# Sparse experts in two phases, tiles turned by DMA flips, one register read per tile

## The reference

```python
x = x + tanh(g_xattn) * attention(layernorm(x), ctx)   # self and cross attention, 16 heads, 8 groups, quantised projections
z = layernorm(x).reshape(2048, 256)
scores = softmax(z @ gate_w.T)                          # 8 experts
topk_w, topk_idx = top_k(scores, 2); topk_w /= topk_w.sum()
y = sum over the 2 experts of topk_w * (silu(z @ w1[e]) * (z @ w3[e])) @ w2[e]    # inner width 176
shared = silu(z @ sw1) * (z @ sw3) @ sw2                # inner width 352
x = x + tanh(g_ffn) * (y + shared)
```

## Time and profile before

| what | value |
|---|---|
| median of 3 runs | 1025.54 us (1023.68 to 1028.03) |
| the profiled execution's own time | 1025.76 us |
| its span, first to last instruction | 1023.9 us |
| mean granted TensorE clock | 0.939 |
| busy share: PE, PEld, DVE, ACT, POOL | 83%, 62%, 76%, 74%, 71% |
| DMA moved | 80.01 MB, mean 78 GB/s |

### The profile page before, as it was taken

The page is one execution under the profiler, slowest core; times in us unless marked ns, Lnnn a source line. Parts: engine busy times, 40 slices in busy tenths (PEclk is TensorE's granted clock), DMA queues, the critical chain, the costliest instruction groups (busy, mean ns, idle before and its releaser), DMA issues. The chain is left out here.

```text
span 1023.9 us, 20898 instructions
## 1 busy us (share of the span) xinstructions
PE 850.3 (83%) x6339; PEld 630.0 (62%) x6339; DVE 778.5 (76%) x1748; ACT 759.8 (74%) x2450; POOL 723.5 (71%) x560
## 2 busy tenths in 40 slices
PE   0475899999999999999999999999866647777841
PEld 0354677777787778777777877778633425555420
DVE  8899888889888898988988888898665764333134
ACT  3486899999999999999999999999772314444210
POOL 4597789799889888888978989888632223332265
PEclk9697899999999999999999999999987769999975
DMA  9423224243333324233332424233534112222134
GB/s 247 106 83 104 57 52 78 53 77 63 62 66 65 73 51 87 51 72 66 61 67 52 87 51 77 62 64 64 145 65 111 53 31 89 91 85 83 47 98 128
DMA packets 191351, 80.01 MB, mean 78 GB/s; under 512 B 168876, under 2 KB 185356, under 8 KB 191308
## 3 DMA queue, kind: packets, MB, share of 16 engines
q1 hardware_dynamic: 183788, 68.07, 29.4%
q0 software_dynamic: 7520, 11.41, 4.7%
HBM read 30.30 MB, written 9.31 MB: 39 GB/s over the span
## 5 line engine op out<-in xcount | busy, mean ns | idle before, releaser
L1609 POOL TENSOR_TENSOR rstd<-var,mhalf 128x8 f32<-128x8 f32 (+1 forms) x128 | 191.2, 1510 | 76.6 <-DVE var L1201 76.2
L386 PE MATMUL A<-w_hi,xq 128*128 128x256 f16 (+1 forms) x1024 | 188.0, 250 | 35.7 <-DVE v_lo L1175 21.2
L387 PE MATMUL A<-w_lo,xq 128*128 128x256 f16 (+1 forms) x1024 | 187.9, 250 | 0.0
L483 PE MATMUL S<-kT,qT 128*128 128x256 f32 x512 | 142.5, 403 | 12.3 <-ACT kT L874 8.9
L1187 DVE TENSOR_SCALAR qT<-T,qmap 128x512 f32<-128x512 f32 x128 | 103.5, 809 | 55.9 <-PE T L454 55.9
L1159 DVE TENSOR_REDUCE nmx<-S 128x2 f32<-128x512 f32 (+1 forms) x192 | 114.8, 598 | 27.8 <-PE S L483 25.6
L885 ACT ACTIVATE prob<-S,nmx 128x256 f32<-128x256 f32 x256 | 119.7, 483 | 14.6 <-DVE nmx L1159 13.5
L386 PEld LDWEIGHTS A<-w_hi,xq 128*128 128x128 f16 x1024 | 101.4, 99 | 46.9 <-issue 30.2
L1673 POOL TENSOR_TENSOR raw<-raw,rstd 128x1024 f32<-128x1024 f32 x64 | 126.5, 1976 | 0.0
L1657 POOL TENSOR_TENSOR prob<-prob,rl 128x1024 f32<-128x1024 f32 x64 | 121.0, 1890 | 0.0
L483 PEld LDWEIGHTS S<-kT,qT 128*128 128x128 f32 x512 | 90.4, 195 | 45.9 <-ACT kT L874 19.4
(11 more groups left out here) (250 smaller groups left out, 2395.9 us busy)
## 6 DMA issues: line engine op xcount, KB each, us to landing
stage<-wallT SPq DMA_DIRECT2D x8, 1024.0 KB, 5.1
yd<-psrc SPq DMA_DIRECT2D x39, 128.0 KB, 1.7
wp<-wpT POOLq DMA_DIRECT2D x1, 2048.0 KB, 30.9
zd<-zf SPq DMA_DIRECT2D x8, 256.0 KB, 2.4
out<-xs SPq DMA_DIRECT2D x8, 256.0 KB
xs<-x SPq DMA_DIRECT2D x1, 1792.0 KB, 21.2
raw<-w13T SPq DMA_DIRECT2D x2, 704.0 KB
sq<-w13T SPq DMA_DIRECT2D x2, 704.0 KB
```

The lines of the kernel that those rows point to most:

```text
L386: nc.tensor.matmul(o, l, w_hi[:, c, col:col + n], start=(c == 0), stop=False)
L387: last = nc.tensor.matmul(o, l, w_lo[:, c, col:col + n], start=False, stop=(c == HC - 1))
L483: last = nc.tensor.matmul(o[:, t * S:(t + 1) * S], qT[:, p, 0, h, t * P:(t + 1) * P], kT[:, p, 0:S], start=True, stop=True)
L1609: return nc.gpsimd.tensor_tensor(dst, src, mhalf[:, 0:n], ALU.pow)
```

## The change

The last batch is taken out of the common plan. **Phase 0** plans, gathers and runs the rows of the first seven batches (NT0 = 35 tiles); **phase 1** those of the last (NT1 = 11 tiles), planned while the tiles of phase 0 run. So there are 46 tiles instead of 39. `yd` becomes two DRAM tensors, one per phase, so that the gathers of the first seven batches' outputs wait for tile 34 and not for the last tile.

**Rows as f16 pairs.** The normalised rows are split before they are stored: ACT's `tail_high` now reads `zf` (which shares `z`'s buffer) and POOL's new `tail_low` subtracts; the pair `zr` is turned by one DMA transpose of 8 blocks and stored to `zd`, 1 KB per row as before (`turn_z(tb)` on SP). PE's `transpose_tokens(zf)` and its waits go.

**Tiles turned by DMA.** Per tile SP issues `flip_z` (4 blocks of 128x128, f16) after the gather, `flip_a` (4 blocks; inner widths 128 and 48 instead of 88 and 88) after silu and the pair split in SBUF, and `store_y`. The PE transposes, `high_z` and `low_z` go. Rings: 6 gathers, 4 flipped z, 3 activation pairs, 4 flipped activations, 4 outputs. The down matmuls follow the up matmuls by DL = 4 tiles.

**One register read.** PE reads the expert number of tile j+1 after `expert_up(j)` and keeps the register until `expert_down` of that tile.

**Order.** POOL's wait for the last attention step ahead of `shared_low(0)` goes (the pair's buffer moved); ranks, tile counts and marks 0 to 7 move into the last attention ticks; `ffn_low(1)` moves two ticks later. In the second half `shared_low` runs on DVE, and POOL issues the 32 output gathers with nothing between them. `mix` no longer waits for `finish`. w2 is padded to 128 rows per half.

```diff
+NT0, NT1 = ((2 * P * n + E * (P - 1)) // P for n in (NE, ST))
+NTL = NT0 + NT1
+PHASES = ((0, NE, 0, NT0), (NE, NT, NT0, NT1))
+DL = 4
...
+            def turn_z(tb):
+                done(sp, ta_lo, tb)
+                sp.dma_start_transpose(zT[:, tb * ST:(tb + 1) * ST, :, :].rearrange("p t k n -> p (t k) n"),
+                                       zr[:, :, :, :].rearrange("p t k h -> p (t k h)")).then_inc(zr_read, 16)
+                sp.dma_start(zd[tb * S:(tb + 1) * S, :].rearrange("(t p) n -> p t n", p=P), zr[:, :, :, :].rearrange("p t k h -> p t (k h)")
+                             ).then_inc(zr_read, 16)
+
+            def flip_z(j):
+                landed(sp, ld_zg, j)
+                done(sp, e_up, j - 4)
+                sp.dma_start_transpose(zt[:, j % 4, :, :], zg[:, j % 6, :]).then_inc(ld_zt[j % 4], 16)
+
+            def flip_a(j):
+                done(sp, e_al, j)
+                done(sp, e_dn, j - 4)
+                sp.dma_start_transpose(at[:, j % 4, :, :], ea[:, j % 3, :, :].rearrange("p k n -> p (k n)")).then_inc(ld_at[j % 4], 16)
+
+            def store_y(j):
+                done(sp, e_y, j)
+                sp.dma_start((yd[0][j * P:(j + 1) * P, :] if j < NT0 else yd[1][(j - NT0) * P:(j - NT0 + 1) * P, :]), yo[:, j % 4, :]).then_inc(st_y[j % 4], 16)
...
+            turn_z(B - 1)
+            for j in range(3): flip_z(j)
+            for j in range(NTL + DL + 1):
+                if j + 3 < NTL: flip_z(j + 3)
+                if j < NTL: flip_a(j)
+                if j - DL + 1 >= 0 and j - DL + 1 < NTL: store_y(j - DL + 1)
...
+            def load_expert(j):
+                if j in (0, NT0):
+                    done(pe, f_idx, j // NT0)
+                which[j] = pe.value_load(expert[0:1, j:j + 1], min_val=0, max_val=E - 1)
...
+            for m in range(3, M0): shared_down(m)
+            load_expert(0)
+            for j in range(NTL + DL):
                 if j < NTL: expert_up(j)
+                if j + 1 < NTL: load_expert(j + 1)
+                if j >= DL: expert_down(j - DL)
+                if j == 2:
+                    pe.wait_ge(zr_read, 16 + 32 * B)
+                    done(pe, d_x1, B - 1)
+                    logits(NE, NT, JB, R_LG - NE * E).then_inc(f_lgm, 1)
+                if j == 7: rank(1)
+                if j == 12:
+                    for t in range(NE, NT): table(1, t)
+                if j == 16: pick_tokens(1)
...
             def high_a(j):
+                done(act, e_a, j)
+                landed(act, ld_at, j - 3)
+                nc.scalar.activation(ea[:, j % 3, 0, 0:I], ap[:, j % 2, :], ACT.Copy).then_inc(e_ah, 1)
...
+            for j in range(NTL + DL):
                 if j < NTL: expert_silu(j)
+                if j >= DL: read_y(j - DL)
+                if j < NTL: high_a(j)
...
             residual(B - 1)
             tail1(B - 1)
-            for t in range(4, 8): marks(t)
+            for t in range(8, NE): marks(t)
+            plan_tiles(0)
             shared_mul(3)
+            read_table(0)
             ffn_low(2)
-            for t in range(8, 12): marks(t)
+            read_tokens(0)
             finish(0)
             ffn_low(3)
...
+            for j in range(NTL):
+                expert_mul(j)
+                low_a(j)
+                if j == 3:
+                    read_logits(1, NE, NT, JB, R_LG - NE * E)
+                    best(1, NE, NT, 0)
+                if j == 4:
+                    best(1, NE, NT, 1)
+                    members(NE, NT)
+                if j == 8: ranks(1)
+                if j == 9:
+                    count_tiles(1)
+                    for t in range(NE, NT): marks(t)
+                if j == 10: plan_tiles(1)
+                if j == 13: read_table(1)
+                if j == 17: read_tokens(1)
+                if j == 18: slots(1)
+                if j == 19: mix_weights(1, NE, NT)
...
-            done(pool, mm_core, STEPS - 1)
             for m in range(3): shared_low(m)
             tail(B - 1)
+            tail_low(B - 1)
             for m in range(3, M0): shared_low(m)
-            exps(1, NE, NT)
-            for j in range(NTL): fetch_z(j)
-            shared_low(M0)
-            shared_low(M0 + 1)
-            for i in range(2 * NT):
-                fetch_y(i)
-                if i % 6 == 3 and M0 + 2 + i // 6 < MS: shared_low(M0 + 2 + i // 6)
+            for j in range(NTL):
+                fetch_z(j)
+                if j == 16: exps(1, NE, NT)
+            for i in range(2 * NT): fetch_y(i)
```

More of the change, by code:

```diff
@@ L657, in rank_late @@
-            def rank_late():
-                done(pe, f_m, 1)
-                for t in range(NE, NT):
-                    nc.tensor.matmul(VB[:, R_CNT:R_CNT + E], all_, member(t, t + 1), start=False, stop=False, skip_group_check=True)
-                rank(VB, NE, NT, False).then_inc(f_rk, 1)
-            def table(t):
+                    nc.tensor.matmul(o(t + 1, t1).rearrange("p (t e) -> p t e", e=E), all_, again(t, t1 - t - 1), start=False,
+                                     stop=False, skip_group_check=True)
@@ L664, in table @@
+                for t in range(t0, t1):
+                    last = nc.tensor.matmul(bank[:, R_CNT:R_CNT + E], all_, member(t, t + 1), start=False, stop=False,
+                                            skip_group_check=True)
+                last.then_inc(f_rk, 1)
+            def table(p, t):
                 done(pe, f_oh, t)
-                if t == 0:
-                    done(pe, a_core, STEPS - 1)
                 for k in range(2):
-                    last = nc.tensor.matmul(VB[:, R_TAB:R_TAB + P], ring[:, t % NR, k, 1, :], ring[:, t % NR, k, 0, :],
-                                            start=(t == 0 and k == 0), stop=False, skip_group_check=True)
+                    last = nc.tensor.matmul((T0, JB)[p][:, R_TAB:R_TAB + P], ring[:, t % NR, k, 1, :], ring[:, t % NR, k, 0, :],
+                                            start=False, stop=False, skip_group_check=True)
@@ L999, in _ @@
                     tick(b, g)
-            def high_z(j):
-                done(act, e_zt, j)
-                done(act, e_up, j - 2)
-                nc.scalar.activation(zt[:, j % 2, 0, :], (JB, VB)[j % 2][:, 0:H], ACT.Copy).then_inc(e_zh, 1)
             def expert_silu(j):
@@ L1260, in tick @@
                         low_px(n0 - 3, par(3))
+                        ranks(0)
+                        count_tiles(0)
                         shared_mul(1)
-                        mix_weights(0, 0, NE)
+                        for t in range(4): marks(t)
                     if g == 3:
@@ L1573, in _ @@
[L1573 to L1588 removed]
+            slots(0)
@@ L1602, in _ @@
             finish(3)
-            for q in range(6, NT // 2): mix(q)
+            for q in range(5, NT // 2): mix(q)
         @block.gpsimd
```

366 lines of the change are left out of this document (153 added, 213 removed).

## The result

The changed kernel took 1043.01 us (median of 4 runs, 1040.05 to 1043.42) beside 1024.97 us for the kernel before in the same measurement: 1.0157 times the time before, 95% interval 1.0139 to 1.0175. The prediction of 989 us (966 to 1018) was wrong in sign and size. The profiled execution has a span of 1041.3 us.

The account below looks back on a forecast made before the run. SP's queue was taken to bound the tile loop at 2.6 us a tile. 1023.9 - 1 + 1.5 - 19 + 13 - 31.6 = 986.8 us of span, plus 1.9 us outside it, gave 989 us, range 966 to 1018.

Parts of the forecast that it names:

- SP's queue: Tile loop: two flips of 1.08 us, a store of 0.32 us and three gaps of 0.05 us, 2.6 us a tile.
- issue equals data: Tile loop: the 20-block flip issues as long as its data takes, so fixed part 0.59 us, 0.123 us a block.
- C: Tile loop, SP's queue: a flip's issue is mostly fixed; at 1.6 us a flip, 1037 us; chance 0.06.
- B: Tile loop: DMA engines or landings decide, 3.1 us a tile, 1012 us; chance 0.17.
- A: Tile loop: PE decides, 2.2 us a tile, 970 us; chance 0.15.
- D: End: the phases do not overlap the end, which keeps some 55 us; 1008 us; chance 0.05.
- The start: Before the tile loop: first up matmul at 820 us, 19 us earlier; 814 to 831.
- the terms for the attention and `turn_z`: Attention: fewer PE transposes gain 1 us; the new 8-block turn in SP's queue costs 1.5 us.
- The gathers under the last tiles: Last seven tiles of the loop: output gathers share the DMA engines, +2 us.
- The way from the last up to the last down: End of the tile loop: four downs and the last activation's way, 5.5 us.
- The end: After the last down: 36 us instead of 67.6, DVE's chain longest, a gain of 31.6 us; 34 to 42.

Follow-up runs that it names:

- the kernel with pairs: Changed kernel with each DMA flip turning two tiles at once and flip_z issued ahead of flip_a; 0.9681 of the kernel before.
- e7_pe_turns_a: Changed kernel with the activations turned by TensorE instead of flip_a, tokens still by flip_z; 0.9673 of the kernel before.
- e9_z_pairs_pe_a: As e7_pe_turns_a, with flip_z turning two tiles at once; 0.9606 of the kernel before, 986.43 us.
- e1_hold: Changed kernel with the first sixteen output gathers waiting for the store of tile 45 instead of tile 34; 1.0065 of the kernel before.
- e3_actstore: Changed kernel with each tile's store issued by ScalarE's queue instead of SP's; 0.9780 of the kernel before.

## Why the prediction was wrong, point by point

**SP's queue, the step that failed.** The prediction found the right bound (SP, ahead of PE and the DMA engines) and gave it 2.6 us a tile; it is 3.23, and 0.5 of the 0.6 us between are two terms that were too small, about half each. The store was taken at 0.32 us, though the row of a plain DMA that follows a flip said 0.59: behind a flip it takes 0.57 us. And the flip: one size was known, 3.06 us for 20 blocks, and the line through it was drawn by an argument (issue equals data, so a fixed part of 0.59 us). Measured are 1.19 to 1.22 us for 4 blocks, 1.23 to 1.28 for 8 in the loop (1.32 in `turn_z`; predicted 1.57), 3.06 for 20. A fixed part and a slope do not fit the three sizes. 20 blocks cost 0.153 us each, 8 at that rate 1.22 us, and 4 cost nearly as much as 8: a floor near 1.2 us fits all three. The rest of the 0.6 us are the gaps between issues, 0.25 us a tile for 0.15. The text gave +41 us for 3.2 us a tile; measured are +39.5. (Its figure for 2.2 us a tile is 13 - 18.4, so -5 and not -6.) The 46 tiles up to the last up matmul take 148.0 us, where the terms sum to 124.6, and the way behind it 8.6 for 5.5. The loop is 26.5 of the 35 us between the predicted span of 986.8 and 1021.9; the start is 5 and the end 3.5 (below).

**The rivals.** C had the mechanism, a flip's issue that blocks do not pay for, with a chance of 0.06. Its break-even of 3.4 us a tile was about right: at 3.29 us the kernel is 0.2% faster. B (DMA engines or landings) had a period near the measured one, 3.1 us, but by another way: they were not the bound of the changed kernel. The DMA engines are the likely next one. Its size was nearly right: 2.2 us a tile predicted, 1.04 x 2.40 = 2.5 us in the kernel with pairs. Against 0.32 x 2.76 = 0.9 us in the one without flips that is 0.20 us for each of the 8 blocks, where 0.17 was taken from the 20-block flip. A (PE decides, 2.2 us) shows only in stretches of e7_pe_turns_a and e9_z_pairs_pe_a (2.24 and 2.25 us), and there PE does four turns a tile besides. D did not occur: 16 gathers ran under the last tiles. The sentence of the Trainium skill that starting a DMA takes little beside the DMA itself ("DMA: Bandwidth & Descriptors", "Issuing engines are not separate DMA queues") does not hold for this loop: moving 0.57 us of issue per tile to another engine's queue was worth 20 us.

**The start.** Predicted 820, measured 825.8, inside 814 to 831; with the terms for the attention and `turn_z`, -18.5 us were predicted and -13.5 measured. POOL's last `shared_low` ended at 819.7, where about 815 was assumed (820 less 5.1), and gather and flip took 5.9 us and not 5.1:

```profile
818.55 1.15 POOL L1731 TENSOR_TENSOR w_hi<-zq,w_hi 96x512 f16<-96x512 f32 x1 [0.71 <-ACT w_hi L807]
...
819.87 1.12 POOL L1738 DMA_INDIRECT w_lo<-zd,w_lo  x1 [0.18 <-issue]
...
822.79 5.03 SPq L358 DMA_TRANSPOSE psrc<-w_lo  x3
...
825.75 0.47 PE L411 MATMUL S<-w_hi,psrc 128*128 x1 [4.51 <-DMA psrc<-w_lo]
```

**The loop's other terms.** The gathers under the last tiles were priced at 2 us and cost 5 (e1_hold). The way from the last up to the last down was priced at 5.5 us; it is 8.6, as the last `flip_a` takes 5.2 us to land (3.5 at the median) where 2.5 was taken.

**The end.** Predicted 36 us (34 to 42), measured 39.5, and 49 in the first measurement. It ends with the gathers' chain and not with DVE's, which was put longest: the last gather is issued at 1014.07 us, lands 3.3 us later, and the last mix, which waits 1.50 us for it, ends at 1019.2:

```profile
1017.43 1.80 DVE L1532 SCALAR_TENSOR_TENSOR xs<-wp,ctx_lo,xs 128x256 f32<-128x256 f32 x4 [1.50 <-DMA wp<-yd,w_lo]
```

The 37.4 us that the mixes waited before are down to 1.5.

**The 18 us of the first measurement.** They are idle times of ScalarE and DVE, most of them under GpSimd's output gathers. That the gathers cause them is not shown: one of 3.94 us lies far ahead of them, and the same gathers, in the same bursts, run without idle times of that size in four other loadings and in the kernels of the table from e3_actstore on. No wait of the program, no instruction load (its DMA packets take 1.7 us at most, and none runs during the two waits of 5.4 and 12.3 us) and no matmul in the trace explains them. The prediction could not have had them, and the cause stays open.

## What to carry to other kernels

Before work is moved from an engine to a DMA queue, add up the issue times of the queue that gets it: a transfer that issues in 1.2 us is dearer than four f16 transposes of 0.06 us on an engine that has idle time in every tile. Take the issue time of a DMA from a row in which its predecessor is the one that it will have, and price an unseen size by both ends, not by a line through one point. In an in-order queue an issue that feeds the next tile belongs ahead of one that waits for this tile (24 us here, for two lines swapped), and a result that hangs on one loading of the program should be measured in a second one before a theory is built on its idle times.

## What the hardware did that was not expected

The issue of a DMA transpose took 1.19 us for 4 blocks, 1.23 for 8 and 3.06 for 20, so halving 8 blocks saved next to nothing. A plain store issues in 0.57 us directly behind a transpose on the same queue and in 0.33 us when the queue was idle before it or is ScalarE's. A store directly behind another store takes 0.44 us at the median (the kernels with pairs). The same program took 1.8% longer in one loading than in four others, while the program it was compared with did not. The granted clock, a mean over its two levels of 1.2 and 2.4 GHz, was 0.79 to 0.83 in the loops of 3.0 to 3.5 us a tile, where PE idles between tiles, and 0.97 to 1.00 in those of 2.4 to 2.8 us (0.89 with single flips and the store on ScalarE's queue). Up matmuls start 0.29 us apart in the slow stretches and 0.15 us apart in the fast ones, so a slower queue cost matmul time too; whether that lengthened the loop, which SP bounds, is not shown.
